# Attention's PSUM banks: two for the maxima and four for the scores, in place of three and three

## The reference, cut to what matters

```
x = _layernorm(x + _L3_attn_ref(x, ...))

q = (x @ wq_w.T + wq_b).reshape(b, t, H, HD)
k1 = (x @ wk_w.T + wk_b); v1 = (x @ wv_w.T + wv_b)      # one head for all 32
scores = jnp.einsum('bqhd,bkd->bhqk', q, k1) / jnp.sqrt(jnp.float32(HD))
causal = jnp.tril(jnp.ones((t, t), dtype=bool))
scores = jnp.where(causal, scores, -jnp.inf)
weights = jax.nn.softmax(scores, axis=-1)
attn = jnp.einsum('bhqk,bkd->bqhd', weights, v1)
return attn.reshape(b, t, H * HD) @ wo_w.T + wo_b
```

## Time and profile before

| | us |
|---|---|
| median of 3 runs (lowest to highest) | 1323.69 (1317.97 to 1324.55) |
| the profiled execution | 1323.85, its span 1322.1 |
| first tile's maxima with the query work | 783 to 847 of the span |
| scores with maxima beside them | 847 to 1067 |
| scores alone, to the last exponential | 1067 to 1122 |

### The profile page before, as it was taken

How to read it: one execution, slowest core, us unless ns; L and a number is a source line. 1 busy time by engine, 2 the same in 40 slices (tenths; PEclk the granted TensorE clock), 3 DMA queues, 4 the chain that set the end, 5 groups by cost and what they waited for, 6 DMA issues and landing times. The chain is left out here.

```text
span 1322.1 us, 14300 instructions
## 1 busy us (share of the span) xinstructions
PE 1241.2 (94%) x5333; PEld 843.1 (64%) x5344; DVE 714.1 (54%) x1186; ACT 437.1 (33%) x747; POOL 162.2 (12%) x215
## 2 busy tenths in 40 slices
PE   7899999899998999998888899899999988999998
PEld 4788688544576788787564445455555533688886
DVE  4321545367748666454343658677767734334344
ACT  2121422111121124222323223466656566222221
POOL 0000000000068200102111220011112224000000
PEclk9999999799999999999977999999999999999999
DMA  8010001733234551103000010000000001022001
GB/s 341 32 49 15 0 1 38 307 127 118 72 109 177 214 214 48 46 0 135 0 0 1 0 48 1 1 1 2 2 2 1 2 3 49 3 94 71 0 25 40
DMA packets 18264, 79.06 MB, mean 60 GB/s; under 512 B 3104, under 2 KB 3872, under 8 KB 16032
## 3 DMA queue, kind: packets, MB, share of 16 engines
q1 hardware_dynamic: 18208, 78.32, 16.4%
HBM read 75.95 MB, written 2.10 MB: 59 GB/s over the span
## 5 line engine op out<-in xcount | busy, mean ns | idle before, releaser
L2348 DVE TENSOR_REDUCE mqa_top<-psum 128x1 f32<-128x512 f32 (+3 forms) x304 | 186.6, 657 | 50.9 <-PE psum L2140 28.4
L2255 ACT ACTIVATE mqa_prob<-psum 128x512 f32<-128x512 f32 x288 | 156.7, 603 | 83.4 <-PE psum L2170 79.4
L587 PE MATMUL psum<-L_ffn_x,L_ffn_w_up 128*128 128x512 f32 x624 | 145.4, 394 | 7.2 <-DVE L_ffn_hidden L740 6.1
L587 PEld LDWEIGHTS psum<-L_ffn_x,L_ffn_w_up 128*128 128x128 f32 x624 | 117.6, 190 | 34.9 <-DVE L_ffn_hidden L740 8.6
L587 PE MATMUL psum<-L_attn_x,L_attn_w_up 128*128 128x512 f32 x456 | 105.4, 393 | 3.9 <-DVE L_attn_hidden L740 3.9
L587 PEld LDWEIGHTS psum<-L_attn_x,L_attn_w_up 128*128 128x128 f32 x456 | 86.6, 190 | 22.5 <-issue 4.3
L2170 PE MATMUL psum<-mqa_stack_back,mqa_keys 100*128 100x512 f32 x208 | 96.2, 462 | 0.9 <-DVE mqa_stack_front L2339 0.9
L2183 PE MATMUL psum<-mqa_prob,mqa_v 128*32 128x512 f32 x576 | 78.4, 609 | 0.0
L117 ACT ACTIVATE ln_std<-ln_mean_var,eps 128x1 f32<-128x1 f32 x56 | 16.5, 295 | 179.2 <-DVE ln_mean_var L104 179.2
L2077 POOL TENSOR_SCALAR_AFFINE_SELECT mqa_prob<-mqa_prob 128x512 f32<-128x512 f32 x64 | 41.7, 671 | 255.5 <-ACT mqa_prob L2255 255.2
L2170 PEld LDWEIGHTS psum<-mqa_stack_back,mqa_keys 100*128 100x128 f32 x208 | 40.0, 192 | 50.2 <-ACT mqa_prob L2255 41.9
(11 more groups left out here) (299 smaller groups left out, 2051.8 us busy)
## 6 DMA issues: line engine op xcount, KB each, us to landing
L_ffn_stage<-in_L_w SPq DMA_DIRECT2D x25, 768.0 KB, 4.7
L_ffn_z_int<-in_L_z SPq DMA_DIRECT2D x14, 768.0 KB, 4.4
L_ffn_s_all<-in_L_s SPq DMA_DIRECT2D x14, 768.0 KB, 6.1
lora_wo<-in_L_wo SPq DMA_DIRECT2D x8, 1024.0 KB, 6.0
L_attn_stage<-in_L_w SPq DMA_DIRECT2D x10, 512.0 KB, 3.5
L_attn_w_down<-in_L_down SPq DMA_DIRECT2D x1, 2560.0 KB, 24.3
x_feat<-in_x_feat SPq DMA_DIRECT2D x2, 1024.0 KB, 6.9
x_tok<-in_x_tok SPq DMA_DIRECT2D x1, 2048.0 KB, 18.7
```

What stands on the lines that cost most here:

```text
L587: ins = nc.tensor.matmul(bank[place][:, :], w_up[:, slot, w_part, at:at + P], x_half[half][:, x_part, k, :], start=k == 0 and n == 0, stop ...
L2255: nc.scalar.activation(prob[:, n % PROBS, :], score_bank[n % 3], ACT.Exp, scale=SCALE)\
L2348: nc.vector.tensor_reduce(top[:, i % 2, 2 if lo == qt * P else lo // HALF, heads[0]:heads[-1] + 1], max_bank[n % 3][:, 0:len(heads) * widt ...
```

## The change

The maxima rotate over two banks (0 and 1), the scores over four (2, 3, 5 and 7). A max matmul now waits for the reduction of the unit two before, a score matmul for the exponential of the score four before. Nothing else differs: the same instructions in the same order on each engine.

```
-        max_bank, score_bank, value_bank = [c.bank[0], c.bank[1], c.bank[7]], [c.bank[2], c.bank[3], c.bank[5]], c.bank[4]
+        max_bank, value_bank = [c.bank[0], c.bank[1]], c.bank[4]
+        score_bank = [c.bank[2], c.bank[3], c.bank[5], c.bank[7]]
...
-                        if n >= 3:
-                            pe.wait_ge(max_taken, n - 2)
+                        if n >= 2:
+                            pe.wait_ge(max_taken, n - 1)
...
-                        out = max_bank[n % 3]
+                        out = max_bank[n % 2]
...
-                        if n >= 3:
-                            pe.wait_ge(exp_ready, n - 2)
+                        if n >= 4:
+                            pe.wait_ge(exp_ready, n - 3)
...
-                        ins = nc.tensor.matmul(score_bank[n % 3], keys[0:SHIFTED, head, cols(kt)],
+                        ins = nc.tensor.matmul(score_bank[n % 4], keys[0:SHIFTED, head, cols(kt)],
...
-                        nc.scalar.activation(prob[:, n % PROBS, :], score_bank[n % 3], ACT.Exp, scale=SCALE)\
+                        nc.scalar.activation(prob[:, n % PROBS, :], score_bank[n % 4], ACT.Exp, scale=SCALE)\
...
-                                                max_bank[n % 3][:, 0:len(heads) * width]
+                                                max_bank[n % 2][:, 0:len(heads) * width]
```

## The result

The changed kernel takes 1349.8 us (median of 4 runs, 1348.94 to 1351.31) against 1320.85 for the kernel before (median of 4): ratio 1.0219, 95% interval 1.0184 to 1.0254. So it is slower clear of the noise, though the interval leaves open whether by a full 2%. Slower was forecast, and the median lies 0.2 us inside the range, at its upper end; two of the four runs lie above it. The profiled execution took 1348.94 us with a span of 1347.2, 25.1 us longer than the span before; the forecast had 19.3.

What follows compares the result with a forecast made beforehand. The prediction took PE's in-order queue as the bound. Terms 17.6 - 0.5 + 4.2 - 2.0 = 19.3 us, added to the profiled 1323.85, gave 1343 us; range 1335 to 1350.

Steps and rivals of the forecast that it cites:

- The middle stage: Attention's second stage, 847 to 1067 us: max loads wait for DVE's reductions, +17.6 us, less 0.5 for waits that vanish.
- Plain rounds: Middle stage, unmasked rounds of 512 columns: third and fourth max wait, values start 0.48 us later; some 25 lose 0.47.
- with head transposes: Middle-stage rounds where head transposes give DVE time: about 0.33 us lost each, 7 rounds counting those with a masked unit.
- of 384 columns: Middle-stage rounds with maxima of 384 columns: 0.32 us lost each, 7 x 0.32 = 2.2 us.
- masked: Middle-stage masked rounds: one bare load, 0.11 us once per round, 14 rounds less a few, 1.4 us.
- those with a projection: Middle-stage plain rounds with a projection standing in them: 4 rounds lose nothing.
- The first stage: Attention's first stage, maxima before any scores: 54 units at 0.08 us, +4.2 us, between 0 and 11.
- only every second pair pays: First stage: a max pair loses 0.32 us but the next pair is free again, giving 0.08 us a unit.
- The last stage: Attention's stage without maxima: fourth score bank saves 0.37 us at nine scores, 3.3 at most; -2.0 us taken.
- the rival with one stretch in four rounds: Clock rival: new waits bring 3.4 us half-clock stretches, one per four of 58 rounds, 24 us on top, 1367; chance 5%.
- Absorbed: Rival: PE's new waits replace other waits and time stays within 0.5%, about 1326 us; chance 4%.
- Faster: Rival: DVE releases banks early enough not to stop PE and the fourth score bank keeps 3.3 us: 1320.5; chance 1%.

Runs made afterwards that it cites:

- e3: Kernel before, with bank 7 given to the scores as a fourth once the maxima are used up; 1322.13 us, ratio 0.9995.
- e2: Changed kernel, but the first tile's 72 maxima rotate over three banks, bank 7 going to the scores afterwards; 1340.74 us, ratio 1.0136 to the kernel before.
- e1: Kernel before with two banks for the maxima in place of three, three for the scores, bank 7 unused; 1349.63 us, ratio 1.0198.
- e6: Changed kernel with every reduction of maxima reading only the first half of each head's keys; 1324.48 us, ratio 1.0018 to the kernel before.
- e7: Kernel before with one bank for the maxima, three for the scores; 1603.9 us, ratio 1.214.
- e8: Kernel before with two banks for the scores in place of three, three for the maxima; 1337.5 us, ratio 1.0097.
- e5: Kernel before (three and three banks) with every reduction of maxima reading only the first half of each head's keys; 1321.65 us, ratio 0.9986.

## Why the prediction was right, and where its sizes were off

**The middle stage** was forecast at +17.6 less 0.5. It is +19.0, of which the clock takes about 1.5: 6.8 us at 1.2 GHz at 1060, after PE had idled for a tile's shift, against 3.4 before.

```profile
1055.00:1060.00 5.00, 3.69 (x21) 1.87 (x20) 3.69 (x8) 2.13 (x5) 2.76 (x4) 1.00 0.00 0
1060.10:1066.90 6.80, 6.80 (x26) 4.58 (x26) 3.66 (x7) 3.03 (x6) 0.00 (x0) 0.50 0.02 6
```

What such a stretch costs, runs with the same code show: the two rounds that hold the one at 979 took 9.92 us in the kernel before and 8.36 in e3, which has none there, 1.6 us; and e2, with 3.4 us in place of 6.8 in the two rounds at 1060, was 1.5 shorter there. That leaves 17.5 for the waits. Plain rounds lost 0.48 (forecast 0.48), with head transposes 0.32 to 0.35 (0.33), of 384 columns 0.31 (0.32), masked 0.12 (0.11), those with a projection 0.00 to 0.02 (0); rounds in which the maxima of a new tile begin behind the shift lost 0.24 to 0.27, which the forecast had not priced by themselves. e1 shows that this comes with the maxima's third bank alone, and e6 that it comes with the time until the reduction releases the bank.

**The first stage** was forecast at +4.2 and is +6.1. One more stretch at 1.2 GHz stands there, 3.4 us at 794, 1.7 us; the waits give 4.4. For the clock's price, this stage took 63.5 us in the kernel before, with one stretch, and 61.8 in e3 with none:

```profile
779.00:841.00 62.00, 55.64 (x194) 31.83 (x195) 48.58 (x86) 19.53 (x32) 0.00 (x0) 1.00 0.00 1
```

The 4.4 agree with the forecast's 4.2, but that sum was rough ("only every second pair pays"), and here nearly every load waits: the size came out in part by luck. e2 takes all of it back.

**The last stage** is the term that was mis-sized: -2.0 forecast, and the fourth bank gives 0.4 (e1 against the changed kernel; 0.8 in the rounds at full clock), though the wait that it was to remove is gone. I had counted nine fourth scores at 0.37 and looked for what absorbs the gain only where the next block's conversions stand. It is also absorbed one step on, by the values waiting for POOL's masking. A second stretch at 1.2 GHz, 1142 to 1145.4, takes 0.9 (as in e1; PE has gaps here that hide part of it), so the stage came out at +0.5.

**The clock.** It has no term in the sum. I gave the rival with one stretch in four rounds 5%, and it did not come. But between 760 and 1155 the changed kernel has 20.4 us at 1.2 GHz against 10.2 before, and they cost about 1.7 + 1.5 + 0.9 = 4.1 us that the sum did not have. With them it closes: waits 4.4 + 17.5, clock 4.1, less 0.4 in the last stage and 0.4 ahead of the attention, 25.2 for 25.1. That the time still fell into the range is luck: its upper end, +25.5, had room for 7 us of waits in the first stage and a last stage without gain, and the clock used that room.
Of the ten profiles, the three with two max banks and whole reductions have 17.0 to 20.4 us there, the six others with two or three max banks 3.4 to 10.2, and e7 262.6 (385.6 to the end of its attention, at 1406). That the clock falls with a PE that idles more shows in e7: the same first two stages have 0.63 and 0.67 in place of 0.97 and 0.99. Whether the 4.1 us follow from the changed kernel's waits is not settled. Against it: e3, with three max banks, has the second stretch of the last stage too, and e8, with three, also has 6.8 us in the middle one.
The waits' own price can be taken apart from the clock by comparing runs with the same mean granted clock. At 0.975 the kernel before took 1324.4 to 1325.5 us and e1 1347.1 and 1347.3, about 22 us apart, against the 21.9 of waits above; at 0.976 to 0.978 e2 lies 16 to 18 us above the kernel before, against 17.5.
The Trainium skill (TensorE: Matmul & The Clock Gate, "A second HAM failure mode: psum-queue depth-cycling") tells of a kernel that cycles through PSUM banks: its PE idles a little between groups of matmuls, and the clock swings between its two levels. The trace of e7 agrees in that the clock swings there (0.67 over the middle stage), with one bank and longer idles; with two banks it hardly shows (0.99 over the middle stage, as before).

**The rivals.** Absorbed: refuted, the plain rounds lost 0.45 to 0.54 us each. Faster: refuted by the load at 863.28. The sum's 19.3 was 6 short of the profiles' 25.1: 4.1 of it is the clock, left outside the sum, 1.6 the last stage, and the rest small differences.

**The runs' medians** are 26 to 29 us apart where the profiles are 25. The kernel before scatters from 1315.3 to 1328.2 over all jobs. The windows ahead of the attention, of e5 and then of e1, show one source: the same 2936 matmuls took 776.9 us at a granted clock of 0.98 and 787.8 at 0.96. That a stage is compared from its own marks keeps this out of the terms above.

```profile
0.00:776.90 776.90, 722.68 (x2936) 513.86 (x2936) 398.52 (x625) 195.94 (x314) 106.99 (x128) 0.98 0.24 89
```
```profile
0.00:787.80 787.80, 736.11 (x2936) 524.65 (x2936) 397.06 (x625) 195.82 (x314) 104.74 (x128) 0.96 0.24 88
```

## What to carry to other kernels

For a rotation of n banks, write one round of the queue down: the writer's issue times, the reader's release times, and compare the release of bank k with the moment the writer comes to bank k + n; if the reader's operation is longer than the writer's pitch (0.60 against 0.47 us here), the bank that let the writer run ahead cannot be taken without stopping the in-order writer in each round, and everything behind it. Check a wait that the profile names by the release time of what it names: most of the 62 us on ACT were no wait for ACT (in the plain round it had ended 0.45 us before the load that is said to wait for it), and a fourth bank left 58.4 of them. Price a bank on both sides before moving it: here the maxima's third was worth 22 us of waits, the scores' third about 14 us (e8), the scores' fourth under 1. A fourth bank for the maxima was not tried.

## What the runs showed of the hardware

- A weight load that waits for a semaphore started 0.05 to 0.06 us after the end of the reduction that releases it, and the next matmul came 0.34 us after it in place of 0.235: the wait costs 0.1 us beyond its own length. In the changed kernel: reduction's end 863.23, load 863.28, next matmul 863.62; the load no longer runs beneath a matmul.
- The clock fell to 1.2 GHz in stretches of 3.4 and 6.8 us, also in the middle of a stage in which PE was busy 96% (232 of 240 us). With PE busy 77% (58 of 75 us) in e7 it stayed there for 75 us.
- A reduction of 512 columns takes 0.68 us, but in a row of four one follows the one before after 0.60 ((2.48 - 0.68) / 3); one of 256 columns took 0.42 (e6).
